# A two-pass graph layer: product 1 of a pair of panels in instructions over both, with two row groups of the next pair ahead of product 2

## What is computed

```
h   = relu(layernorm(x))                     # x: 5120 x 64
e   = h + par0*par1 * ((diag * h) @ W)       # first 2048 rows with one set of weights, the rest with another
h2  = adj @ (adj.T @ e)                      # adj: 5120 x 5120, fp32, 105 MB
out = x + layernorm(h2) * gamma + beta + h
```

## Time and profile before

| what | value |
|---|---|
| median of three runs | 378.31 us (377.38 to 378.63) |
| the profiled execution | 378.12 us, span 376.2 us |
| PE busy | 367.9 us, 98% of the span |
| PEld / DVE / ACT / POOL busy | 193.5 / 253.1 / 73.3 / 23.2 us |
| matmul records: product 1, product 2 with strips, with cols | 1600, 2432, 160 |
| DMA | 133.13 MB, 354 GB/s on average |
| mean granted clock of TensorE | 0.995 of full speed |

### The profile page before, as it was taken

One profiled execution on the slowest core, in us unless ns is written; L12 is line 12 of the kernel. 1 busy time (PEld: TensorE's weight loads), 2 busy tenths in 40 slices (PEclk: granted clock), 3 DMA queues, 4 the chain that ended last, 5 costly groups with the idle time before them and its releaser, 6 DMA issues.

```text
span 376.2 us, 9721 instructions
## 1 busy us (share of the span) xinstructions
PE 367.9 (98%) x4328; PEld 193.5 (51%) x4328; DVE 253.1 (67%) x242; ACT 73.3 (19%) x212; POOL 23.2 (6%) x29
## 2 busy tenths in 40 slices
PE   7998999999999999999999999999999999999994
PEld 5764454545643663465456436634654464456332
DVE  5999995859628933993497279439933982632476
ACT  4853022100220032003102200220022023002321
POOL 2039000000000000000000000000000000000035
PEclk9999999999999999999999999999999999999997
DMA  8999999999999999599959986995999699949003
GB/s 310 420 416 424 416 422 420 422 416 424 421 416 423 355 429 421 225 416 428 421 184 416 427 369 271 425 423 226 362 425 424 226 421 428 384 151 407 4 12 129
DMA packets 19602, 133.13 MB, mean 354 GB/s; under 512 B 2176, under 2 KB 2560, under 8 KB 3712
## 3 DMA queue, kind: packets, MB, share of 16 engines
q1 hardware_dynamic: 19296, 132.48, 85.9%
q10 hardware_dynamic: 288, 0.39, 0.3%
HBM read 131.55 MB, written 1.31 MB: 353 GB/s over the span
## 4 chain that ended last, share of the span: by engine, by line
PE 89%; DVE 6%; ACT 2%; issue 1%; DMA 1%; DVEq 0%
PE t_acc L635 42%; PE h_acc L664 35%; PE h_acc L648 9%; DVE strips L453 2%; ACT strips L325 2%; PE h_acc L623 1%; PE t_acc L701 1%; DVE var L416 1%; PE h_acc L612 1%; DMA xs<-x 1%; DVE scaled L577 1%; DVE centred L411 0%; DVE natural L561 0%; PE h_acc L715 0%; DVE scaled L570 0%
## 5 line engine op out<-in xcount | busy, mean ns | idle before, releaser
L453 DVE STREAM_TRANSPOSE strips<-natural 128x2048 f32<-128x2048 f32 x76 | 168.2, 2276 | 49.4 <-PE h_acc L664 49.3
L635 PE MATMUL t_acc<-natural,e 128*64 128x256 f32 x1600 | 176.0, 380 | 0.7 <-DMA natural<-adj_rows 0.5
L635 PEld LDWEIGHTS t_acc<-natural,e 128*64 128x64 f32 x1600 | 114.2, 137 | 63.6 <-issue 6.5
L664 PE MATMUL h_acc<-strips,centred 32*64 32x512 f32 x2432 | 133.3, 589 | 0.6 <-DVE strips L453 0.6
L664 PEld LDWEIGHTS h_acc<-strips,centred 32*64 32x64 f32 x2432 | 53.4, 132 | 78.8 <-issue 77.9
L333 ACT COPY t_high<-t_acc 64x256 f32<-64x256 f32 x20 | 7.4, 368 | 211.7 <-PE t_acc L635 211.7
L461 DVE TENSOR_TENSOR t_sum<-t_acc,t_high 64x256 f32<-64x256 f32 x20 | 8.2, 410 | 56.3 <-ACT t_high L333 56.0
L648 PE MATMUL h_acc<-cols,centred 128*64 128x512 f32 x160 | 38.3, 599 | 0.0
L340 ACT COPY centred<-centred 32x384 f32<-32x384 f32 (+2 forms) x60 | 24.2, 403 | 68.3 <-DVE centred L474 67.9
L341 ACT COPY centred<-centred 32x128 f32<-32x128 f32 (+2 forms) x60 | 23.9, 398 | 0.0
L288 POOL TENSOR_TENSOR scaled<-scaled,smalls 128x512 f32<-128x512 f32 x2 | 2.5, 1268 | 325.8 <-DVE scaled L577 325.8
(11 more groups left out here) (53 smaller groups left out, 77.4 us busy)
## 6 DMA issues: line engine op xcount, KB each, us to landing
natural<-adj_rows SPq DMA_DIRECT2D x100, 1024.0 KB, 11.5
cols<-adj_cols SPq DMA_DIRECT2D x20, 1024.0 KB, 13.2
natural<-adj_last SPq DMA_DIRECT2D x4, 1024.0 KB, 6.2
out<-xs SPq DMA_DIRECT2D x5, 256.0 KB, 2.0
xs<-x SPq DMA_DIRECT2D x3, 256.0 KB, 6.3
xs<-x ACTq DMA_DIRECT2D x1, 256.0 KB, 3.9
smalls<-small SPq DMA_DIRECT2D x1, 214.5 KB, 3.6
xs<-x ACTq DMA_DIRECT2D x1, 128.0 KB, 2.9
```

What stands on the lines that cost most here:

```text
L453: nc.vector.transpose(strips[:, a, :, m].rearrange("p c t i -> p t c i"), natural[:, a, m].rearrange("p t (c j) -> p t c j", j=Q)).then_in ...
L635: last = nc.tensor.matmul(t_acc[D * s:D * (s + 1), a, 0:WIDE], e[:, GT * m + 2 * k + s, :], natural[:, a, m, HALF * s + k], start=(m == 0 ...
L664: last = nc.tensor.matmul(h_acc[D * s:D * (s + 1), q], t[part, a, b, u, :], rows, start=(isinstance(g, int) and g == 0 and b == 0 and u == 0),
```

## The change

Product 1 of the pairs (panels 4 to 17) is made by `first_pair`: one matmul streams 256 columns of each of the two panels, 512 in all, into a full PSUM bank. `t_acc` has two banks as before; a pair has one bank, and successive pairs alternate (`t_place`). Each row group now waits for the loads of both panels, and `s_first` is raised by 2.

PE's order changes too. `first_pair` of pair 2 (panels 4, 5) is made whole, ahead of the loop. Then each turn of the loop does, twice: the first two row groups (`EARLY`) of the next pair, product 2 of this pair, the other three row groups of the next pair. The loop turns three times and covers panels 4 to 15 in its product 2; panels 16 and 17 stand behind it, with four row groups of panel 18 (256 wide, panel 18 alone) ahead of their product 2.

The order of the loads is new from panel 6 on: two row groups of g, cols of g - 2 and g - 1, two row groups of g + 1, then (g, 2), (g, 3), (g + 1, 2), (g + 1, 3), (g, 4), (g + 1, 4). Panels 18 and 19 are loaded one after the other. The columns of panels 4 and 5 in `cols` thus stand behind (6, 0) and (6, 1).

DVE and ACT keep their order within a pair; ACT waits for the first product of the whole pair before the first `t_high`.

```diff
+QUADS = 4
+EARLY = 2
...
         def pairs(eng, pair):
-            with eng.Fori(PAIRED // 2, PANELS // 2 - 1) as i:
-                pair(2 * i, i)
-            pair(LAST - 1, LAST // 2)
+            with eng.Fori(1, QUADS) as i:
+                for c in range(2):
+                    pair(4 * i + 2 * c, 2 * i + c, c)
+            pair(LAST - 3, LAST // 2 - 1, 0)
...
+        def firsts_pair(half, m):
+
+            return 2 * (GROUPS * half + m + 1)
+
+        def t_place(c, a):
+
+            return c, slice(WIDE * a, WIDE * (a + 1))
+
+        def t_single(g, a):
+
+            return 1 - a if g >= LAST - 1 else a, slice(0, WIDE)
...
-            for g in range(2, PANELS):
-                if g > PAIRED and g % 2 == 0:
-                    sp.wait_ge(s_loaded_done, g - 2)
-                    load_cols(g - 1)
+
+            def refill(g, m):
+                if g < 4:
+                    sp.wait_ge(s_first, firsts_0(g - 2, m))
+                elif g < PAIRED + 2:
+                    sp.wait_ge(s_first, firsts(g - 2, m))
+                else:
+                    sp.wait_ge(s_first, firsts_pair(g // 2 - 1, m))
+                if m < TURNED:
+                    sp.wait_ge(s_strips, TURNED * (g - 2) + m + 1)
+                load_natural(g, m)
+
+            def refill_cols(g):
+                sp.wait_ge(s_loaded_done, g - 1)
+                load_cols(g)
+
+            for g in range(2, PAIRED + 2):
                 for m in range(GROUPS):
...
+                    refill(g, m)
                 if g == 2:
                     load_cols(1)
                 if g < PAIRED:
...
+                    refill_cols(g)
+            for g in range(PAIRED + 2, PANELS, 2):
+                for m in range(EARLY):
+                    refill(g, m)
+                for a in range(2):
+                    refill_cols(g - 2 + a)
+                if g < LAST - 1:
+                    for m in range(EARLY):
+                        refill(g + 1, m)
+                    for ms in ((2, 3), (4,)):
+                        for a in range(2):
+                            for m in ms:
+                                refill(g + a, m)
+                else:
+                    for m in range(EARLY, GROUPS):
+                        refill(g, m)
+                    for m in range(GROUPS):
+                        refill(g + 1, m)
+            refill_cols(LAST - 1)
...
-            def both_first(g, half):
-                for a in range(2):
-                    for m in range(GROUPS):
-                        first(g + a, a, half, m)
-
-            def pair(g, half):
-                both_first(g, half)
+            def first_pair(half, c, ms):
+
+                for m in ms:
+                    for a in range(2):
+                        pe.wait_ge(s_natural[a][m], 16 * (half + 1))
+                    if m == 0:
+                        if isinstance(half, int):
+                            pe.wait_ge(s_t_sum, PAIRED - 1)
+                        else:
+                            pe.wait_ge(s_t_sum, 2 * half - 2)
+                    for k in range(HALF):
+                        for s in range(2):
+                            last = nc.tensor.matmul(t_acc[D * s:D * (s + 1), c].rearrange("p (a w) -> p a w", a=2),
+                                                    e[:, GT * m + 2 * k + s, :], natural[:, :, m, HALF * s + k],
+                                                    start=(m == 0 and k == 0),
+                                                    stop=(m == GROUPS - 1 and k == HALF - 1))
+                    last.then_inc(s_first, 2)
+
+            def second_pair(g, half):
                 second_loaded(g, 0, half)
...
-            with pe.Fori(PAIRED // 2, PANELS // 2 - 1) as i:
-                pair(2 * i, i)
-            both_first(LAST - 1, LAST // 2)
+            first_pair(PAIRED // 2, 0, range(GROUPS))
+            with pe.Fori(1, QUADS) as i:
+                for c in range(2):
+                    first_pair(2 * i + c + 1, 1 - c, range(EARLY))
+                    second_pair(4 * i + 2 * c, 2 * i + c)
+                    first_pair(2 * i + c + 1, 1 - c, range(EARLY, GROUPS))
+            for m in range(2 * EARLY):
+                first(LAST - 1, 0, LAST // 2, m)
+            second_pair(LAST - 3, LAST // 2 - 1)
+            for m in range(2 * EARLY, GROUPS):
+                first(LAST - 1, 0, LAST // 2, m)
+            for m in range(GROUPS):
+                first(LAST, 1, LAST // 2, m)
```

More of the change, by code:

```diff
@@ L327, in layer_input, with keep_t_high @@
                 last.then_inc(s_h, 1)
-            def keep_t_high(g, a, done):
+            def keep_t_high(g, place, done):
+                bank, columns = place
                 act.wait_ge(s_first, done)
@@ L332, in keep_t_high @@
                     act.wait_ge(s_t_sum, g)
-                nc.scalar.copy(t_high[:], t_acc[D:2 * D, a, 0:WIDE]).then_inc(s_t_high, 1)
+                nc.scalar.copy(t_high[:], t_acc[D:2 * D, bank, columns]).then_inc(s_t_high, 1)
             def spread_t(g, a):
@@ L344, in step, with pair @@
             def step(g, a, half):
-                keep_t_high(g, a, firsts(g, GROUPS - 1))
+                keep_t_high(g, t_single(g, a), firsts(g, GROUPS - 1))
                 spread_t(g, a)
-            def pair(g, half):
+            def pair(g, half, c):
                 for a in range(2):
-                    step(g + a, a, half)
+                    keep_t_high(g + a, t_place(c, a), firsts_pair(half, GROUPS - 1))
+                    spread_t(g + a, a)
             square(0)
@@ L376, in _ @@
             for g in range(2):
-                keep_t_high(g, g, firsts_0(g, GROUPS - 1))
+                keep_t_high(g, t_single(g, g), firsts_0(g, GROUPS - 1))
                 spread_t(g, g)
@@ L381, in _ @@
             pairs(act, pair)
+            for a in range(2):
+                step(LAST - 1 + a, a, LAST // 2)
             def square_out(m):
@@ L454, in turn_strips, with keep_t @@
                                     natural[:, a, m].rearrange("p t (c j) -> p t c j", j=Q)).then_inc(s_strips, 1)
-            def keep_t(g, a):
+            def keep_t(g, a, place):
                 dve.wait_ge(s_t_high, g + 1)
@@ L460, in keep_t @@
                     dve.wait_ge(s_t_part, g)
-                nc.vector.tensor_tensor(t_sum[:], t_acc[0:D, a, 0:WIDE], t_high[:], ALU.add).then_inc(s_t_sum, 1)
+                bank, columns = place
+                nc.vector.tensor_tensor(t_sum[:], t_acc[0:D, bank, columns], t_high[:], ALU.add).then_inc(s_t_sum, 1)
                 dve.wait_ge(s_t_sum, g + 1)
@@ L479, in step, with pair @@
                     turn_strips(g, a, half, m)
-                keep_t(g, a)
-            def pair(g, half):
+                keep_t(g, a, t_single(g, a))
+            def pair(g, half, c):
                 for a in range(2):
@@ L486, in pair @@
                 for a in range(2):
-                    keep_t(g + a, a)
+                    keep_t(g + a, a, t_place(c, a))
             def deviation(u):
@@ L536, in _ @@
             turn_strips(0, 0, 0, 2)
-            keep_t(0, 0)
+            keep_t(0, 0, t_single(0, 0))
             turn_strips(0, 0, 0, 3)
@@ L540, in _ @@
                 turn_strips(1, 1, 0, m)
-            keep_t(1, 1)
+            keep_t(1, 1, t_single(1, 1))
             for g in range(2, PAIRED):
                 step(g, g % 2, g // 2)
-            with dve.Fori(PAIRED // 2, PANELS // 2 - 1) as i:
-                pair(2 * i, i)
+            pairs(dve, pair)
             for m in range(TURNED):
                 turn_strips(LAST - 1, 0, LAST // 2, m)
-            keep_t(LAST - 1, 0)
-            keep_t(LAST, 1)
+            keep_t(LAST - 1, 0, t_single(LAST - 1, 0))
+            keep_t(LAST, 1, t_single(LAST, 1))
             dve.wait_ge(s_strips_last, 1)
@@ L630, in first @@
                     pe.wait_ge(s_natural[a][m], 16 * (half + 1))
-                if m == 0 and not (isinstance(g, int) and g < 2):
-                    pe.wait_ge(s_t_sum, g - 1)
+                if m == 0 and g >= 2:
+                    pe.wait_ge(s_t_sum, g - 2 if g == LAST - 1 else g - 1)
+                bank, columns = t_single(g, a)
                 for k in ks:
                     for s in range(2):
-                        last = nc.tensor.matmul(t_acc[D * s:D * (s + 1), a, 0:WIDE], e[:, GT * m + 2 * k + s, :],
+                        last = nc.tensor.matmul(t_acc[D * s:D * (s + 1), bank, columns], e[:, GT * m + 2 * k + s, :],
                                                 natural[:, a, m, HALF * s + k],
```

4 lines of the change are left out of this document (removed).

## The result

The changed kernel takes 382.53 us as the median of six executions (381.38 to 384.23), before 378.21 in the same comparison: ratio 1.0123, 95% interval 1.0105 to 1.0142. It is slower, as forecast, but by 4.3 us and not by 1.4; 382.53 lies outside the range that ended at 381.3.

The account below looks back on a forecast made before the run. The prediction took PE's own instruction stream as the bound. A 0.7 us gain and a 2.1 us stall summed to +1.4 us: 379.5 against the profiled execution, stated as 379.7 against the 378.31 median, range 377.3 to 381.3.

Parts of the forecast that it names:

- the sum's second term: At the loop's start, PE waits for (7,0), landing at 107.4 against 105.3 us: one stall of 2.1 us.
- the upper bound of 3.0: Largest stall allowed at the loop's start, in us, if a load's isolated latency is 5.5 us and not 4.7.
- The spare for (a = 1, m = 0): In the steady loop, this load lands at 25.9 us after product 2's start, about 1.5 us early, every pair.
- the stall repeats: Rival: (1, 0) lands 2 us later in every pair, about 0.5 us wait in six further pairs: 382.7 us; chance 0.08.
- Part 3: The order of the loads: landing times in the steady loop and at its start, where it expected a 2.1 us stall.
- The gain: Product 1 of the seven pairs: 512-column slots of 0.429 us save 0.10 us a pair, 0.7 us in all.
- the estimate after the spacings of the Trainium skill: Two 256-column matmuls cost about 195 ns against 131 for one of 512, so product 1 loses a third of 121 us.
- The cover by two row groups: Ahead of product 2, 6.87 us of row groups cover the 5.55 us chain to t: no wait.
- The end: At the last panels, four row groups of panel 18 (6.9 us) cover t's 5.55 us: nothing added to PE's end.
- Code loading: Rival: the longer loop body no longer stays resident, each of two jumps back waits 2.0 us: 383.7 us; chance 0.06.
- the forecast's own range: For the case of one stall of 1.5 to 3.0 us at the loop's start: 378.9 to 380.6 us; chance 0.64.

Follow-up runs that it names:

- e11: The changed kernel itself, unaltered, timed once more beside the fill: 382.64 us.
- e8: The changed kernel with one row group ahead of product 2 instead of two, and both `cols` load reorderings (early first two, later odd panel): 394.48 us, ratio 1.0431.
- the fill: The changed kernel plus 24 matmul records on zeros into an unused PSUM bank, between `first_pair(2)` and the loop; run twice: 382.03 and 380.64 us.
- e1: The changed kernel with only the `cols` loads of panels 4 and 5 moved back ahead of (6,0): 377.97 us, ratio 1.0001.
- e12: Second run of the fill, beside the changed kernel: 380.64 us.
- e4: First run of the fill: 382.03 us, ratio 1.0092.
- e13: The changed kernel with both `cols` load reorderings, and panels 6 and 7 loaded in the order (6,0), (7,0), (6,1), (7,1): 376.84 us, ratio 0.9977.
- e3: The narrow kernel: the changed kernel with each wide matmul made as two of 256 columns, same order, waits and loads: 406.82 us, ratio 1.0742.
- e10: The kernel before with only PE's loop body doubled (two pairs a turn, three turns, seventh pair written out): 383.53 us, ratio 1.0144.

## Why the prediction was wrong in size

**The step that failed** is the sum's second term, "So the stall is 107.4 - 105.3 = 2.1 us". It priced the stall as idle time and nothing else. The place, the loads in front of (7,0) and the order of events were right, and so was the direction. In the profile of the changed kernel the place cost 5.0 us: 3.25 of stall, and 1.74 of lower clock behind it, which the prediction puts at nothing. The median is 2.8 us over the forecast, which is the size of that missing term and of the 1.2 us that the stall was longer.

- *The stall.* Counted from the start of `first_pair(2)`, (7,0) was to land after 19.2 us. In the first profile it landed after 20.15, since (6,0) took 6.6 and (6,1) 5.7 us where I had taken 4.7 for a load with an empty queue; why they took longer in this execution isn't shown. In the repeated profile (e11) they took 4.8 and 4.9, (7,0) landed after 19.35, and the stall was 2.46 us. PE restarted 0.3 us after the landing in both, and not at once. So the term was short by 1.2 us in one execution and by 0.4 in the other; the upper bound of 3.0 held for one of the two.
- *The clock.* It isn't in the sum, the rivals or the bounds. The clock row of before showed no fall in the loop, and I read that as a constant, though PE had no stall of this length there to test it. The two profiles of the stall, with the fall and without it, the six stalls of e8 and the executions with the fill show that the fall goes with the stall, in some executions and not in others. A low mean can have other causes: e1's 0.992 does, and two of the 23 executions of before beside e1 have 0.989 and take 380.28 and 380.66 us, with no profile of theirs on record.
- *The spare for (a = 1, m = 0)*, "about 1.5 us, every pair". It is none: the load issued at 136.97 lands 7.7 us later, at 144.7, which is 28.0 us after product 2's start and not 25.9. That gave waits of 0.43, 0.52 and 0.15 us, 1.1 in all. In the profiles of e11, e12 and e4 the same load lands 27.5, 27.7 and 28.6 us after it, with a wait of none, none and 0.80 us. The rival "the stall repeats" was the right mechanism and came true by a third. Part 3 added 2.49 us for each load behind the first; the steps to the second `cols` and to this load were 3.2 and 3.3 us, for a reason that the runs don't show.
- *The gain.* Forecast 0.7 us, slot 0.429. Measured 34.77 to 34.67 in a pair, 3.433 a row group, 0.9 us between e13 and before. Right, and the estimate after the spacings of the Trainium skill ("TensorE: Matmul & The Clock Gate", section "Back-to-back issue gap"; a third off product 1) is not borne out here: two widths, one price per column within 1%.
- *The cover by two row groups.* Right: no wait for t in the changed kernel, and 2.3 us in each of six pairs with one row group.
- *The end* is unchanged: right. *Code loading* didn't happen in the changed kernel: 18 packets in all for a longer program, and none in the second turn. Of the figures of the Trainium skill ("Runtime: NRT & Kernel Launch", section "Instruction fetch mechanics"), the 2,048 instructions would let the body of 1,728 pass, which was fetched again here (e3 and e10); two pages would not have let 1,408 pass. The runs put the limit between the two bodies, counted in matmuls and weight loads; the waits and the other instructions of a body come on top.

The ledger of the profile: 0.7 us gained; 3.25 + 1.74 + 1.10 lost; `first_pair(2)` started 0.47 us earlier. That is +4.9, and the two spans differ by 5.0. For the repeated profile it is 0.7 gained and 2.46 lost, with `first_pair(2)` 1.30 us later: +3.1, and its span is 379.3. It took 381.09 us; without that late start it would be 379.8, against the 379.7 forecast: where the clock stayed up and no later pair waited, the sum was nearly right.

A slip in the forecast's own range: with 378.31, less 0.7 and with a stall of 1.5, its lower end is 379.1 and not 378.9.

## What to carry to other kernels

When an instruction comes to need two buffers at once, or a step is moved ahead, redo the landing time of every load that it waits for where the queue changes regime, at a loop's first turn above all, and order the queue by need: here the place of two loads was worth 4.6 us and the new instruction 0.7. Price a stall of 2 us or more on TensorE with the clock that may fall behind it. Count the instructions of a loop's body before it is doubled: here the wide instructions, with 1,408 in place of 1,728, are what let the doubled body turn without a stop. And where a short gap is put down to "issue", compare it with the landing of the load behind the next wait.

## Not expected of the hardware

- The granted clock fell to its lower level (0.57 on average over 4.0 us, 1.7 us lost) after idle stretches of 2.0 us (e8), 2.1 (e8) and 3.25 (the changed kernel), and not after four others of 2.0 to 2.1 in the same execution of e8, nor after one of 2.46 in another execution of the changed kernel.
- A loop body of 1,408 matmuls and weight loads turned without new instruction packets. One of 1,728 was fetched again in every turn and lost 2.6 us (in the kernel before, doubled) or 11.4 us (in the narrow kernel) at each jump back. Written out without jumps, the same instructions came in 34 packets and cost no stop.
- Two runs of 256 columns from different buffers in one moving operand cost nothing: 3.433 us a row group is the step of 0.429 that the single-buffer matmuls have the earlier trace rows.
